# A decoder layer on one core: the middle heads of TensorE as a loop, level 16 of a block inverse on two 64x64 tiles, and three steps moved

## The reference

```python
x = x + _L0_attn_ref(_layernorm(x), ...)    # gated delta rule, 16 heads of 128
x = x + _L0_xattn_ref(_layernorm(x), ctx)   # attention map of the context, applied to tokens
x = x + _L0_ffn_ref(_layernorm(x), ...)     # top-1 of 8 low-rank experts
```

```python
M = M * jnp.exp(g_t)[..., None, None]
Mk = jnp.einsum('bhd,bhdv->bhv', k_t, M)
M = M + jnp.einsum('bhd,bhv->bhdv', k_t, (v_t - Mk) * b_t[..., None])
o_t = jnp.einsum('bhd,bhdv->bhv', q_t, M)
```

## Time and profile before

| | us |
|---|---|
| median of 3 runs | 2038.53 (2036.16 to 2044.75) |
| the profiled execution, its own time | 2033.38 |
| its span, first to last instruction | 2031.7 |
| PE busy | 1915.2 (94% of the span) |
| DVE, ACT, POOL busy | 1128.8, 934.1, 743.1 |
| mean granted clock of TensorE | 0.958 |

### The profile page before, as it was taken

The page is one execution under the profiler, slowest core; times in us unless marked ns, Lnnn a source line. Parts: engine busy times, 40 slices in busy tenths (PEclk is TensorE's granted clock), DMA queues, the critical chain, the costliest instruction groups (busy, mean ns, idle before and its releaser), DMA issues.

```text
span 2031.7 us, 45678 instructions
## 1 busy us (share of the span) xinstructions
PE 1915.2 (94%) x16962; PEld 1561.4 (77%) x16962; DVE 1128.8 (56%) x2048; ACT 934.1 (46%) x2987; POOL 743.1 (37%) x1143
## 2 busy tenths in 40 slices
PE   5899999999999999999999998999997799999999
PEld 3688888888888888888888887888886565656574
DVE  5656565665656575656656665657563442534433
ACT  2455554646464555646464645555563321213121
POOL 1255453636363554536363535445452000000000
PEclk9899998999998999989999999989997899999999
DMA  3011111112010111111120101021114513121110
GB/s 101 16 33 32 33 40 25 34 30 42 22 38 22 38 32 33 39 25 37 28 43 22 38 22 38 23 41 34 31 24 144 146 36 93 42 83 52 55 27 21
DMA packets 220196, 87.10 MB, mean 43 GB/s; under 512 B 138320, under 2 KB 204240, under 8 KB 219280
## 3 DMA queue, kind: packets, MB, share of 16 engines
q1 hardware_dynamic: 220048, 84.83, 16.4%
HBM read 57.28 MB, written 27.53 MB: 42 GB/s over the span
## 4 chain that ended last, share of the span: by engine, by line
PE 49%; issue 25%; POOL 10%; DVE 7%; ACT 4%; DMA 3%; SPq 1%; POOLq 1%; DVEq 0%; ACTq 0%
PE bank L558 17%; PE bank L858 4%; PE bank L808 3%; DVE vT L1406 2%; POOL blkT L1774 2%; PE bank L817 2%; PE bank L770 2%; POOL prod L1770 2%; PE bank L759 2%; PE bank L678 2%; ACT vv L1074 2%; PE bank L802 2%; POOL k_tok L1740 2%; PE bank L824 1%; DMA blkT_d<-blkT 1%
## 5 line engine op out<-in xcount | busy, mean ns | idle before, releaser
L558 PE MATMUL bank<-x_hi,w_hi 128*128 128x512 f32 x1024 | 433.5, 423 | 13.4 <-DVE vT L1406 7.1
L558 PE MATMUL bank<-x_hi,w_lo 128*128 128x512 f32 x1024 | 410.3, 401 | 0.0
L558 PE MATMUL bank<-x_lo,w_hi 128*128 128x512 f32 x1024 | 408.7, 399 | 1.1 <-issue 1.1
L558 PEld LDWEIGHTS bank<-x_hi,w_hi 128*128 128x128 f32 x1024 | 197.9, 193 | 56.1 <-issue 13.9
L558 PEld LDWEIGHTS bank<-x_hi,w_lo 128*128 128x128 f32 x1024 | 196.7, 192 | 43.8
L558 PEld LDWEIGHTS bank<-x_lo,w_hi 128*128 128x128 f32 x1024 | 197.7, 193 | 33.2 <-issue 1.6
L1406 DVE SCALAR_TENSOR_TENSOR qT<-bank,cw,qT 128x511 f32<-128x511 f32 (+2 forms) x192 | 142.1, 747 | 51.1 <-ACT qT L1041 46.5
L1830 POOL TENSOR_TENSOR rstd<-ve,mhalf 128x1 f32<-128x1 f32 x32 | 17.4, 544 | 386.8 <-DVE ve L1588 386.8
L1406 DVE SCALAR_TENSOR_TENSOR kT<-bank,cw,kT 128x511 f32<-128x511 f32 (+2 forms) x192 | 143.3, 747 | 9.9 <-ACT kT L1041 4.9
L1206 ACT ACTIVATE o_tmp<-bank 128x128 f32<-128x128 f32 x256 | 67.4, 278 | 175.5 <-PE bank L824 175.5
L1406 DVE SCALAR_TENSOR_TENSOR vT<-bank,cw,vT 128x511 f32<-128x511 f32 (+2 forms) x192 | 143.2, 746 | 6.8 <-ACT vT L1041 2.3
(11 more groups left out here) (221 smaller groups left out, 4446.2 us busy)
## 6 DMA issues: line engine op xcount, KB each, us to landing
w_raw<-in_w_heads SPq DMA_DIRECT2D x64, 256.0 KB, 2.8
o_d<-og SPq DMA_DIRECT2D x64, 256.0 KB, 2.6
o_raw<-o_d SPq DMA_DIRECT2D x16, 1024.0 KB, 6.2
x_in<-in_x SPq DMA_DIRECT2D x16, 256.0 KB, 3.3
blkN_d<-nT SPq DMA_DIRECT2D x64, 64.0 KB, 2.1
t<-blkT_d SPq DMA_DIRECT2D x64, 64.0 KB, 2.4
wo_raw<-in_w_out SPq DMA_DIRECT2D x4, 1024.0 KB, 9.1
x_res<-in_x SPq DMA_DIRECT2D x16, 256.0 KB, 2.7
```

The lines of the kernel that those rows point to most:

```text
L558: last = mm(bank[bk][:, :], w[:, kind % 2, d, :], xx[:, d, b * S:(b + 1) * S], start=(n == 0), stop=(n == 3 * ND - 1))
```

## The change

1. PE's heads 1 to 14 are a loop; heads 0 and 15 stay written out.
2. Level 16 works on two 64x64 tiles instead of four 32x32 ones: 32 products where there were 64, for y as for z, each 32 columns wide. DVE alone applies the result, to `t32` (four instructions, masked by a vector `late_rows`, with the negative sign in it), and then transposes `t32` into `tT` again. `join32_y` waits for `z16_done` and no longer for these transposes; `join32_z` waits for them.
3. PE's order in the join: `join16_y` stands before `qk(1)`, both `join32_y` in front, the filling products 2, 3, 2, 3, 2; the second group's y64 products alternate with the first group's z64 products.
4. The last gating of a head is done on DVE at step `c == 2` of the next, and the split of the z weights after `nT[3]`.
5. Two of the four loads of `t32` are issued by ACT, after `z_silu(3)`.
6. On ACT, copies of the join go ahead of two taps of the next head's convolution.

```diff
-JOIN_FILL = (7, 2, 2, 1)
+JOIN_FILL = (2, 3, 2, 3, 2)
...
-    TILE_BANK = (2, 3, 4, 6)
...
+    HALF_TILES = [EARLY, LATE]
+    Y16_BANK, Z16_BANK = (2, 3), (4, 6)
+
+    def block16(t, which):
+
+        return t.rearrange("p (j k s) -> p j k s", j=2, k=2)[:, :, which, :]
...
# sync engine, head()
                 sp.wait_ge(blkT_out, 32 * h + 32)
-                for k in range(NPAIR):
+                for k in range(NPAIR // 2):
...
# tensor engine, head()
-                            for j, t in enumerate(TILES):
-                                s = slice(t.start, t.start + BLK)
-                                last = mm(tiny(j, t, 0, c, b), nT[s, b, c, t], t32[s, b, c, s], start=True, stop=True)
+                            for i, t in enumerate(HALF_TILES):
+                                last = mm(half16(Y16_BANK[i], t, c, b), nT[t, b, c, t], block16(t32[t, b, c, t], 0),
+                                          start=True, stop=True)
                     last.then_inc(y16_mm, 1)
 
                 def join16_z():
                     pe.wait_ge(y16_done, h + 1)
-                    pe.wait_ge(tT_done, 4 * h + 4)
+                    pe.wait_ge(tT_done, 8 * h + 4)
...
+                            for i, t in enumerate(HALF_TILES):
+                                last = mm(half16(Z16_BANK[i], t, c, b), tT[t, b, c, t], y16[t, b, c, :], start=True, stop=True)
...
                 def join32_y(g):
 
-                    pe.wait_ge(t32_done, 4 * h + 2 * g + 2)
+                    pe.wait_ge(z16_done, h + 1)
...
                 def join32_z(g):
                     pe.wait_ge(y32_done, 2 * h + g + 1)
+                    pe.wait_ge(tT_done, 8 * h + 4 + 2 * g + 2)
...
+                def join64_both():
+
+                    pe.wait_ge(z32n_done, 2 * h + 2)
+                    pe.wait_ge(y64_done, 2 * h + 1)
+                    pe.wait_ge(z32_done, 2 * h + 1)
                     hold(pe, "pe")
...
+                    for i, b in PAIRS:
+                        y_last = y64_product(1, i, b)
+                        z_last = z64_product(0, i, b)
+                    y_last.then_inc(y64_mm, 1)
+                    z_last.then_inc(z64_mm, 1)
...
                 qk(0)
+                join16_y()
                 qk(1)
-                join16_y()
                 ahead(JOIN_FILL[0])
                 join16_z()
                 qk(2)
                 qk(3)
+                join32_y(0)
+                join32_y(1)
                 ahead(JOIN_FILL[1])
-                join32_y(0)
+                join32_z(0)
                 ahead(JOIN_FILL[2])
-                join32_y(1)
-                join32_z(0)
+                join32_z(1)
+                join64_first()
                 ahead(JOIN_FILL[3])
-                join32_z(1)
-                join64_y(0)
-                join64_y(1)
-                join64_z(0)
-                join64_z(1)
+                join64_both()
+                ahead(JOIN_FILL[4])
+                join64_last()
...
-            for h in range(H):
-                head(h, h == 0, h < H - 1)
+            head(0, True, True)
+            with pe.Fori(1, H - 1) as h:
+                head(h, False, True)
+            head(H - 1, False, False)
...
# scalar engine, head()
-                    for j, t in enumerate(TILES):
-                        last = fn(y16[t, :, :, :], tinies(j, t, 0), ACT.Copy)
+                    for i, t in enumerate(HALF_TILES):
+                        last = fn(y16[t, :, :, :].rearrange("p b c s -> p (b c) s"), halves16(Y16_BANK[i], t), ACT.Copy)
...
+                act.wait_ge(blkT_out, 32 * h + 32)
+                for k in range(NPAIR // 2, NPAIR):
+                    sl = slice(k * PAIR, (k + 1) * PAIR)
+                    act.dma_start(t32[sl, :, :, sl].rearrange("t b c s -> t (b c) s"),
+                                  blkT_d[k].rearrange("u t s -> t u s")).then_inc(t32_in, 16)
                 keep16_y()
...
-                join16()
+                keep32_y(0)
+                keep32_y(1)
                 if more:
...
                     tap(h + 1, K_, 0)
-                keep32_y(0)
-                keep32_y(1)
                 keep32_n(0)
                 keep32_n(1)
+                keep64_y(0)
+                keep64_y(1)
                 if more:
                     tap(h + 1, K_, 1)
-                keep64_y(0)
-                keep64_y(1)
...
# vector engine, head()
+                    if c == 2 and not first:
+                        gated(h - 1, NC - 1)
                     if c == 3:
                         ts(k_sqe[:, :, :], k_sq[:, :, :], EPS_L2, None, ALU.add).then_inc(kvec_step, 1)
-                        split(h, Z_)
...
-                if not first:
-                    gated(h - 1, NC - 1)
+                split(h, Z_)
...
+                for j, t in enumerate(TILES):
+                    early = t32[t, :, :, t.start:t.start + BLK].rearrange("p b c s -> p (b c) s")
+                    last = stt(early, halves16(Z16_BANK[j // 2], t)[:, :, j % 2 * BLK:j % 2 * BLK + BLK], late_rows[t, :], early,
+                               ALU.mult, ALU.add)
                 last.then_inc(z16_done, 1)
-                dve.wait_ge(z16_done, 2 * h + 2)
+                dve.wait_ge(z16_done, h + 1)
                 for c in range(NC):
-                    nc.vector.transpose(t32[:, :, c, :], tT[:, :, c, :]).then_inc(t32_done, 1)
+                    nc.vector.transpose(tT[:, :, c, :], t32[:, :, c, :]).then_inc(tT_done, 1)
```

More of the change, by code:

```diff
@@ L156, in layer @@
     gt = [gt_0, at(place["y1"][0], "gt_1", [P, 2, B, P], F32R)]
-    y16 = at(place["y1"][0], "y16", [P, NC, B, BLK])
+    y16 = at(place["y1"][0], "y16", [P, B, NC, PAIR])
     y32 = at(place["gt_0"][0], "y32", [P, NC, B, PAIR])
@@ L749, in join32_z, with y64_product @@
                     last.then_inc(z32_mm, 1)
-                def join64_y(g):
-                    pe.wait_ge(z32n_done, 2 * h + g + 1)
-                    if g == 0:
-                        pe.wait_ge(pT_done, 4 * h + 4)
-                    hold(pe, "pe")
-                    for i in range(2):
-                        for b in range(B):
-                            c = 2 * g + i
-                            last = mm(large(half_bank(g), LATE, i, b), nT[EARLY, b, c, LATE], t32[EARLY, b, c, EARLY],
-                                      start=True, stop=True)
+                def y64_product(g, i, b):
+                    c = 2 * g + i
+                    return mm(large(half_bank(g), LATE, i, b), nT[EARLY, b, c, LATE], t32[EARLY, b, c, EARLY], start=True, stop=True)
@@ new lines, in z64_product, with join64_first @@
+                def z64_product(g, i, b):
+                    c = 2 * g + i
+                    return mm(large(half_bank(g), EARLY, i, b), y64[LATE, c, b, :], tT[LATE, b, c, LATE], start=True, stop=True)
+                PAIRS = [(i, b) for i in range(2) for b in range(B)]
+                def join64_first():
+                    pe.wait_ge(z32n_done, 2 * h + 1)
+                    pe.wait_ge(pT_done, 4 * h + 4)
+                    hold(pe, "pe")
+                    for i, b in PAIRS:
+                        last = y64_product(0, i, b)
@@ L772, in join64_z, with join64_last @@
+                def join64_last():
+                    pe.wait_ge(y64_done, 2 * h + 2)
+                    pe.wait_ge(z32_done, 2 * h + 2)
+                    hold(pe, "pe")
+                    for i, b in PAIRS:
+                        last = z64_product(1, i, b)
                     last.then_inc(z64_mm, 1)
                 qk(0)
+                join16_y()
                 qk(1)
-                join16_y()
                 ahead(JOIN_FILL[0])
@@ L1694, in _ @@
             chain(memset(minus_half[:, :], -0.5))
+            for t in TILES:
+                chain(memset(late_rows[t, :], -1.0))
+                chain(memset(late_rows[t.start:t.start + BLK, :], 0.0))
             chain(memset(half[:, :], 0.5))
```

41 lines of the change are left out of this document (9 added, 32 removed).

## The result

| | before | changed |
|---|---|---|
| median of 3 runs, us | 2038.53 | 2078.74 (2077.34 to 2098.33) |
| the profiled execution, its own time | 2033.38 | 2098.33 |
| mean granted clock | 0.958 | 0.938 |

The ratio is 1.022 with a 95% interval of 1.0143 to 1.0296. The forecast was 2017 us, with a range of 1968 to 2065. The profile belongs to the longest of the three executions.

The account below looks back on a forecast made before the run. PE, 94% busy, was taken to be bound by its work, idle time and clock. Loop heads of 91.9 us against 93.2 save 18 us, heads 0 and 15 perhaps 3: 2012 profiled, 2017 as median; range 1968 to 2065.

Parts of the forecast that it names:

- 87.0: A loop head before pause and fall: 88.0 us, less 0.5 for the join and 0.5 for v.
- The pause: At level 16 PE waits 2.6 us in every head for ACT's late loads of t32; bounds 1.0 to 4.3.
- The fall: Behind the pause at level 16 the clock drops, costing 2.3 us a head, taken from falls of 1.8 and about 3.5.
- a sign of its being wrong: The forecast is wrong if, among other signs, the clock is down for over 5 us a head.
- The better case: Rival at level 16: ACT issues ahead of its arithmetic, wait 1.0 us, fall 0.9, 88.9 us a head, 1975; chance 0.20.
- The join: From t32's landing to the inverse: DVE's chain sums to 14.1 us against 14.6 today, 0.5 us saved a head.
- the tail is untouched: The part of the kernel behind the heads was taken as unchanged, with no gain or loss.
- The loop: PE's 1,700 instructions of a head stay on chip; 13 of 14 loop heads fetch nothing, fetch gaps and long falls go.
- The move of the gating: Gating costs DVE nothing before nT[2]; SP's blkN_d goes 2.2 us earlier, and POOL's chain with it.
- the 0.5 us for `vT`: The convolution of v ends up to 0.5 us earlier, removing a wait of 0.5 us a head.
- The two rivals of 2077: Either the wait moves to the join's end with a clock fall, chance 0.13, or the loop isn't kept, chance 0.08.
- gains promised in heads 0 and 15: In the two written-out heads, shorter code and join32_y without transposes in front give perhaps 3 us.

Follow-up runs that it names:

- a1_sp_loads: The changed kernel with all four loads of t32 issued by SP again, none by ACT: 2004.63 us, ratio 0.9858.
- d1_banks: a1_sp_loads with level 16's banks exchanged and PE's waits for the last squares and scaled v moved to the second products: 1974.72 us, ratio 0.9709.
- a3: a1_sp_loads with PE's heads written out instead of looped: 2012.42 us, ratio 0.9892.
- c1_loop_from_2: a1_sp_loads with the loop over heads 2 to 14 and head 1 written out too: 2018.71 us, ratio 0.9922.
- d2: a1_sp_loads with level 64 not in turns, second group's y64 products before first group's z64: 2016.35 us, ratio 0.9904.
- d5: a1_sp_loads with the first products of level 16 on half of their data columns, 16 instead of 32: 2018.59 us.
- d4: a1_sp_loads with the first products of level 16 on half of their weights, 64x32 instead of 64x64: 1981.94 us.
- b1_loop: The kernel before the change with one edit, PE's heads 1 to 14 as a loop: 2095.68 us, ratio 1.0274.

## Why the prediction was wrong, by its steps

A loop head was forecast as 87.0 + 2.6 (pause) + 2.3 (fall) = 91.9 us. Measured is 96.2, the mean of the 13 stretches from 228.81 to 1479.21. The price of a short fall is 1.6 us (92.0 against 90.4 in a1_sp_loads), so the changed kernel's head without one is 91.3, and it splits as 89.2 + 2.1 + 4.9.

- **The fall (2.3 taken, 4.9 measured)** is the step that failed most, 36 us over 14 heads. It was taken from the two rows where a pause at level 16 stood ahead, and the falls of 5 us were ascribed to late packets alone. In the changed kernel the same pause is followed by falls that cost 1.6 to 10 us, and the clock is down for 11 us a head on average, where the prediction named 5 us as a sign of its being wrong. All six such pauses in the trace before had cost 1.8 or 3.4 us, so more of its rows would not have shown the long falls: a price taken at the old level 16 did not hold at the new one. What decides the length stays open.
- **The pause (2.6 taken, 2.1 measured)** and its cause were right: ACT's issue was late, `blkN_d` went 0.1 us behind `nT`, and SP's own loads were early. Not seen: with `qk(1)` gone from the front, the squares alone make PE wait 1.13 us, so loads in time don't end the pause. The better case allowed for 1.0 us of this, but its 1975 didn't follow either: with the loads in time a1_sp_loads took 2004.63.
- **The join (0.5 us saved, over 2 lost).** The passes of level 16 were sized by their number. But each took three times as long, by wider weights and fewer tiles in turns: 0.8 us more for y and for z, where 0.25 less each was taken. From level 16 to the first product with the inverse d1_banks takes 16.7 us, where 14.1 were summed. The DVE chain was not the bound; PE waited 0.18 us for it, ahead of level 32.
- **Head 15.** Its loads were not looked at: "the tail is untouched" was true of the code, not of the queue ahead of ACT's issue. 15.8 us of pause more than in a loop head, and some 5 us in the tail, which began at half clock.
- **The loop** was kept and the fetch gaps ended, as forecast. But with the heads written out the gaps would have ended too, but for a few us.
- **The move of the gating**, and the 0.5 us for `vT`: right.
- **The two rivals of 2077** have the measured time by accident: no pause at the end of the join was there, and the loop was kept.

In sum, against the profiled execution: 14 x 4.3 = 60 us for the heads, 16 for head 15, 5 for the tail, 3 for gains promised in heads 0 and 15: 84 of the 86 us between 2012 and 2098.

## What to carry to other kernels

Price a pause of TensorE by the fall that can stand behind it, not by its length, and don't carry the price over to other products behind the pause: here 2.1 us of pause cost 7 us on average, and an exchange of banks, which removed a pause of 1.13 us, gave 1.5%. When cover is moved away from a wait, look for every event that it covered, not just the latest one. And before a loop replaces written-out code, count the blocks of instructions that its body touches, where it starts included.

## What the runs showed of the hardware that was not expected

- After a pause of 2.1 us ahead of small products the granted clock fell in every loop head and stayed at 0.50 for 3.4 to 23.9 us. The length went with the moment at which the fall began: 12 of 12 that began 0.88 to 1.04 us into level 16 lasted 23.9 us, 28 of 28 that began at 1.36 us or later 3.4 us. After 1.13 us it fell in 3 to 13 of 15 heads (a1, a3, c1, d2, d5), and in none of heads 1 to 13 where the passes behind the pause took 1.2 us instead of 2.1 (d4). After 1.6 to 1.9 us ahead of large products (c1_loop_from_2) it fell once in 12 times.
- A loop body across seven blocks of 256 instructions was kept whole (no packet from 261 to 1532 us), across eight it was fetched whole in every round (nine packets each in b1_loop and c1_loop_from_2).
- With small products, the columns of the weights and the number of tiles in turns went with the length of TensorE's pass: with two tiles 32 ns for 64 columns and 19 for 32, with four tiles and 32 columns 10. Halving the data columns, 32 to 16, changed 33.3 us to 33.2.
- ACT sent the second of its transfers 1.1 us before the silu that stands ahead of them in its program began (998.59 against 999.70), with a group of four squares also still to start.
